# A decoder block on one core: the three joints of the feed-forward part reworked, and one difference moved to GpSimd

## The chip, the core and the metric

The kernel runs on one core of a Trainium2 chip. TensorE multiplies matrices (page name PE, its weight loads PEld), VectorE (DVE), ScalarE (ACT) and GpSimd (POOL) do the elementwise work, SyncE (SP) issues the DMAs. The engines run their own instruction lists and meet only at semaphores. The metric is the device time of one execution in microseconds, lower is better.

## The reference

For x of 16 x 128 x 1024 values in float32, a pre-norm decoder block:

```python
x = x + attn(layernorm(x), Wqkv, q_ln, k_ln, Wout)     # 32 heads, alibi bias, causal, clipped qkv
x = x + xattn(layernorm(x), ctx, Wq, Wk, Wv, Wo, bo, g) # linear attention over channels
W1, W3, W2 = [dequant_q40(w, s) for each]               # two 4-bit values a byte, a scale per group of 64
a = x_n @ W1.T; b = x_n @ W3.T                          # x_n = layernorm(x), 2752 hidden units
x = x + (silu(a) * b) @ W2.T
```

## The kernel before

The program has three phases, each a block of instructions with a barrier behind it: the qkv product, attention (both attentions and Wout, `attention_phase`), and the feed-forward part (`feed_forward_phase`), which the change is about.

Attention goes through the 16 row blocks in turns. Turn b holds the first attention of block b, the second of block b - 1, and the norm, transposes (`post_turn`) and store to `xt` of block b - 2. The last turn, turn 16, has only the second attention of block 15 (`own` is false); the norm and store of block 15 stand behind the turns, and SyncE waits for that store before the block ends.

The feed-forward part splits each float32 operand into a high and a low half and multiplies high by high, high by low and low by high: a product is 12 matmuls of 512 columns. The rows are taken in two halves of 1024. In each half there are 21 whole tiles of 128 hidden units and one merged tile that holds the last 64 units of w1 and w3 together. For a whole tile the 2 by 2 block product is made with seven products instead of eight (A11, S1, S2, A12, S3, S4, A22, in this order): the left operands are blocks and sums of blocks of the weights (GpSimd forms the sums in `left_sums`, ScalarE copies them as high halves into a ring of ten places, DVE subtracts for the low halves), and the right operands b11, t1, t2, b21, t3, b22, t4 are blocks and differences of blocks of the rows, formed once a half (`start_half`, `right_sums`) from `raw`, 4 MB of rows loaded from `xt`. `t1` = R12 - R11 is DVE's, the other three differences are GpSimd's. The merged tile has two products of length 24 and 36 matmuls on b11, t1, b21 and b22. Their places, and those of w2 and of the outputs, lie over one another, so a semaphore guards each reuse.

While TensorE works on tile u, DVE unpacks the weights of tile u + 1 (`unpack13`: two shifts and two scalings), makes its low halves, adds the partial sums of tile u in four `combine`s, and gates. TensorE's second product of tile u + 1 waits for the third `combine` of tile u. After the merged tile of the second half, w2 is loaded and unpacked (`load2`, `unpack2`), split (`w2_high`, `w2_low`), the hidden rows come back from `hid` (`load_hidden`, `hidden_high`, `hidden_low`), `acc` is loaded with the residual rows, and 24 groups of eight output products follow; sum n into `acc` is added by DVE in `add`, and the bank of product n is used again by product n + 8.

Three joints are thus: attention to the first half, first half to second half (in `start_half(1)`), second half to the outputs. The order on each engine is written out by hand.

## Time and profile before

| | |
|---|---|
| median of 3 runs | 3293.26 us (3288.9 to 3293.31) |
| the profiled execution | 3291.72 us, its span 3289.7 us |
| mean granted TensorE clock | 0.968 of full speed |
| busy: PE, DVE, ACT, POOL | 3027.4, 1808.2, 1178.8, 940.9 us |
| first feed-forward load issued | at 1859.12 us |

Busy shares are means over stages with different limits. The stages to look at are the stretches in which TensorE does nothing between two trains of products. A timeline row gives start, duration, engine, line, operation and tiles (output first), the number of instructions merged, and in brackets the idle time before it and what ended it.

### The profile page before, as it was taken

The numbers are of one execution on the slowest core, as the hardware profiler recorded it, in microseconds if no ns is written. First come the engines' busy times: TensorE is split into PE (matmuls) and PEld (weight loads), VectorE is DVE, ScalarE is ACT, GpSimd is POOL, SyncE is SP. The second block draws the span as 40 slices with busy tenths as digits, with TensorE's granted clock in tenths as the row PEclk, the third lists the DMA queues.
The fourth block names the chain that finished last, engine by engine and source line by source line (L and its number), as shares of the span: only waits on it lengthen the run. The fifth ranks groups of instructions, "written<-read, shape, count | busy, mean of one in ns | idle before, by whom it ended". The sixth has DMA issues, their size and how long they took to land. (4 is left out here: it accounts for less than half of the span.)

```text
span 3289.7 us, 40227 instructions
## 1 busy us (share of the span) xinstructions
PE 3027.4 (92%) x14656; PEld 2308.0 (70%) x14656; DVE 1808.2 (55%) x2933; ACT 1178.8 (36%) x2618; POOL 940.9 (29%) x781
## 2 busy tenths in 40 slices
PE   7999998799999999999998389999699996999999
PEld 6888886566666666666655178888588885788887
DVE  5311112466666666666665476665766664455543
ACT  2100000566666665566564233333333332111110
POOL 2100000233333333333343433332533331212221
PEclk9999999899999999999999689999899998999999
DMA  4222222111111111111110222222323224633323
GB/s 144 93 71 74 70 77 101 57 36 48 45 51 46 56 45 54 48 45 45 45 54 30 93 77 84 95 93 77 113 84 103 85 84 116 212 103 94 99 60 119
DMA packets 103341, 256.88 MB, mean 78 GB/s; under 512 B 12352, under 2 KB 18496, under 8 KB 101184
## 3 DMA queue, kind: packets, MB, share of 16 engines
q1 hardware_dynamic: 103232, 255.39, 23.8%
q8 instruction: 72, 1.18, 0.1%
q14 instruction: 37, 0.30, 0.0%
HBM read 181.95 MB, written 73.40 MB: 78 GB/s over the span
## 5 line engine op out<-in xcount | busy, mean ns | idle before, releaser
L1536 PE MATMUL ff_room<-xy,ring_hi 128*128 128x512 f32 x1424 | 358.8, 395 | 40.4 <-DVE xy L1406 25.0
L1536 PEld LDWEIGHTS ff_room<-xy,ring_hi 128*128 128x128 f32 x1424 | 271.3, 191 | 99.1 <-issue 32.9
L284 DVE TENSOR_SCALAR qkv_out<-qkv_acc 128x512 f32<-128x512 f32 x96 | 66.4, 692 | 395.2 <-PE qkv_acc L314 395.2
L1536 PE MATMUL ff_room<-xz,ring_hi 128*128 128x512 f32 x1008 | 252.5, 393 | 29.4 <-DVE xz L1406 29.4
L1445 DVE TENSOR_TENSOR acc<-ff_room,acc 128x512 f32<-128x512 f32 x192 | 130.6, 691 | 227.6 <-PE ff_room L314 220.2
L711 ACT ACTIVATE scores<-scores,neg_max 128x128 f32<-128x128 f32 x512 | 199.2, 390 | 134.0 <-DVE neg_max L496 134.0
L1536 PEld LDWEIGHTS ff_room<-xz,ring_hi 128*128 128x128 f32 x1008 | 191.2, 190 | 70.1 <-issue 30.3
L1410 DVE TENSOR_TENSOR ends<-ends,ff_room 128x512 f32<-128x512 f32 x168 | 115.5, 687 | 212.3 <-ACT ends L1261 198.4
L314 PE MATMUL ff_room<-w_hi,h_hi 128*128 128x512 f32 x704 | 193.4, 393 | 35.2 <-DVE w_lo L1437 28.7
L1226 POOL TENSOR_TENSOR h_lo<-hraw,h_hi 128x2048 fp32r<-128x2048 f32 (+1 forms) x24 | 101.6, 4232 | 413.9 <-ACT h_hi L1322 413.9
L1261 ACT ACTIVATE ends<-ff_room 128x512 f32<-128x512 f32 x126 | 75.3, 598 | 388.4 <-PE ff_room L1536 388.4
L754 POOL TENSOR_TENSOR scores<-scores,row_rec 128x512 f32<-128x512 f32 x128 | 133.3, 1041 | 268.2 <-DVE row_rec L824 268.2
L314 PE MATMUL qkv_acc<-w_hi,xT_hi 128*128 128x512 f32 x768 | 193.0, 394 | 8.9 <-DVE w_lo L257 8.9
L233 ACT ACTIVATE w_hi<-w_stage 128x512 fp32r<-128x512 f32 x56 | 35.4, 632 | 452.9 <-DMA w_stage<-in_w_attn 452.9
L314 PE MATMUL ff_room<-w_lo,h_hi 128*128 128x512 f32 x704 | 192.5, 392 | 0.0
L314 PE MATMUL ff_room<-w_hi,h_lo 128*128 128x512 f32 x704 | 192.5, 392 | 0.0
L1536 PE MATMUL ff_room<-xy,ring_lo 128*128 128x512 f32 x712 | 192.1, 392 | 0.0
L314 PE MATMUL qkv_acc<-w_lo,xT_hi 128*128 128x512 f32 x768 | 190.0, 389 | 0.0
L314 PE MATMUL qkv_acc<-w_hi,xT_lo 128*128 128x512 f32 x768 | 189.8, 389 | 0.0
L314 PEld LDWEIGHTS ff_room<-w_hi,h_hi 128*128 128x128 f32 x704 | 133.9, 191 | 63.8 <-issue 29.0
L1367 DVE TENSOR_SCALAR words<-words,shift 128x1024 int32<-128x1024 int32 (+1 forms) x130 | 143.0, 1113 | 58.5 <-DMA sc<-in_s 43.3
L765 POOL TENSOR_TENSOR qr<-qr,q_rec 128x512 f32<-128x512 f32 x128 | 133.7, 1044 | 139.7 <-DVE q_rec L802 139.7
(179 smaller groups left out, 6260.3 us busy)
## 6 DMA issues: line engine op xcount, KB each, us to landing
words<-in_w SPq DMA_DIRECT2D x86, 512.0 KB, 4.8
qkv<-qkv_out SPq DMA_DIRECT2D x96, 256.0 KB, 2.0
hid<-ends SPq DMA_DIRECT2D x88, 256.0 KB, 3.3
hraw<-hid SPq DMA_DIRECT2D x20, 1024.0 KB, 5.1
qk_in<-qkv SPq DMA_DIRECT2D x16, 1024.0 KB, 4.9
w_stage<-in_w_attn SPq DMA_DIRECT2D x56, 256.0 KB, 3.0
words<-in_w SPq DMA_DIRECT2D x88, 128.0 KB, 3.5
sc<-in_s SPq DMA_DIRECT2D x44, 256.0 KB, 4.0
```

What stands on the lines that cost most here:

```text
L233: nc.scalar.activation(dst[:, r, :], stage[:, r % 2, :], ACT.Copy).then_inc(w_hi_done, 1)
L284: nc.vector.tensor_scalar(res[:, :], acc[:, t % BANKS, :], CLIP, -CLIP, ALU.min, ALU.max).then_inc(clipped, 1)
L314: last = nc.tensor.matmul(out, left, right, start=n == 0, stop=n == len(pairs) - 1)
L711: last = nc.scalar.activation(sc[:, t % SR, j, :], sc[:, t % SR, j, :], ACT.Exp, bias=neg_max[:, t, j:j + 1], accum_out=row_sum[:, t, j:j ...
L754: nc.gpsimd.tensor_tensor(sc[:, n % SR, :, :], sc[:, n % SR, :, :], row_rec[:, n, :].unsqueeze(2).to_broadcast([P, HG, P]), ALU.mult).then ...
L765: nc.gpsimd.tensor_tensor(q, q, q_rec[:, n, :].unsqueeze(2).to_broadcast([P, 8, XD]), ALU.mult).then_inc(s["q_normed"], 1)
L1226: nc.gpsimd.tensor_tensor(flat(h_lo[m % 2][:, 0:n, :]), flat(hraw[m % 2][:, 0:n, :]), flat(h_hi[m % 2][:, 0:n, :]).bitcast(F32), ALU.subtr ...
L1261: nc.scalar.activation(ends[u % 2][:, n, :], chain[u % 2], ACT.Copy).then_inc(s["snapped"], 1)
L1367: last = nc.vector.tensor_scalar(w[:, at], w[:, at], shift[:, 2 * kind:2 * kind + 1], shift[:, 2 * kind + 1:2 * kind + 2], ALU.logical_shi ...
L1410: nc.vector.tensor_tensor(e, e, other, ALU.add).then_inc(s["combined"], 1)
L1445: nc.vector.tensor_tensor(columns(t, n % 2), bank(o), columns(t, n % 2), ALU.add).then_inc(s["added"], 1)
L1536: last = nc.tensor.matmul(out.rearrange("p (a b) -> p a b", a=SETS), l, r, start=not onto and n == 0, stop=n == len(pairs) - 1, skip_group ...
```

## The change

The feed-forward part's helper functions move out of its block. Its first operands are loaded, unpacked and formed in attention's last turn, by `enter_sync`, `enter_gpsimd`, `enter_scalar` and `enter_vector`, which `turn_*` call where `own` is false; attention's tiles are placed anew so that the two do not overlap. The norm, transposes and store of row block 15 move behind that: into the first tiles of the first half (`finish_*`). b11 of the second half has places of its own (`spare`); the merged tile's two products change places; the weights of the second half's first tile are prepared during the tile before the merged one. In the first half all four differences are DVE's; in the second half `t3` is GpSimd's (`difference3_gpsimd`) and the other three DVE's. Of w2's blocks four have a buffer each, and they, the first hidden rows and six `acc` tiles are loaded before the merged tile. High and low left operands share one tile, `ring`. `unpack13`, `left_sums`, `left_high` and `left_low` stay as they were apart from their place in the program. The core of the diff (changes of indentation are left out):

```diff
+        if not own:
+            sp.wait_ge(s["x_done"], 2 * NB)
+            sp.wait_ge(s["xt_stored"], HALF * 16)
+            enter_sync(sp)
...
+            enter_scalar(act, 0)
...
+            enter_gpsimd(pool)
...
-            post_store(sp, NB + 1)
-            sp.wait_ge(s["stored"], (NB + 1) * 16)
-            sp.wait_ge(s["xt_stored"], NB * 16)
...
+    spare = [place(f"xs{i}", [P, SETS, HK, P], F32R, (190 + 8 * i) * KB) for i in range(2)]
...
-    b11, b21, b22, t1 = [(plain[2 * i], plain[2 * i + 1]) for i in range(4)]
-    t2, t3, t4 = (zone[0], zone[1]), (zone[3], zone[5]), (zone[2], zone[4])
-    right = [b11, t1, t2, b21, t3, b22, t4]
+    b11 = [(plain[0], plain[1]), (spare[0], spare[1])]
+    b21, b22, t1 = [(plain[2 * i], plain[2 * i + 1]) for i in range(1, 4)]
+    t2, t3, t4 = (zone[0], zone[1]), (zone[2], zone[5]), (zone[3], zone[4])
...
+    def difference1(dve, hf):
+        for at in (R11, R12):
+            dve.wait_ge(r_in[at - R21], (hf + 1) * 64)
+        nc.vector.tensor_tensor(raw[:, 0, :], raw[:, R12, :], raw[:, R11, :], ALU.subtract).then_inc(s["x_t1"], 1)
+
+    def difference2(dve, hf):
+        dve.wait_ge(s["x_t1"], hf + 1)
+        dve.wait_ge(r_in[R22 - R21], (hf + 1) * 64)
+        nc.vector.tensor_tensor(raw[:, 1, :], raw[:, R22, :], raw[:, 0, :], ALU.subtract).then_inc(s["x_t"], 1)
+
+    def difference4(dve, hf):
+        dve.wait_ge(s["x_t"], 2 * hf + 1)
+        dve.wait_ge(r_in[0], (hf + 1) * 64)
+        nc.vector.tensor_tensor(raw[:, R11, :], raw[:, R21, :], raw[:, 1, :], ALU.subtract).then_inc(s["x_t"], 1)
+
+    def difference3(dve, hf):
+        nc.vector.tensor_tensor(raw[:, R12, :], raw[:, R22, :], raw[:, R12, :], ALU.subtract).then_inc(s["x_t3"], 1)
+
+    def difference3_gpsimd(pool, hf):
+        pool.wait_ge(s["x_t1"], hf + 1)
+        pool.wait_ge(r_in[R22 - R21], (hf + 1) * 64)
+        nc.gpsimd.tensor_tensor(raw[:, R12, :], raw[:, R22, :], raw[:, R12, :], ALU.subtract).then_inc(s["x_t3"], 1)
...
+        op, at = [(b11[hf], R11), (t1, 0), (t2, 1), (b21, R21), (b22, R22), (t3, R12), (t4, R11)][n]
+        if n == 0:
+            act.wait_ge(r_in[R11 - R21], (hf + 1) * 64)
+        elif n == 1:
+            act.wait_ge(s["x_t1"], hf + 1)
+            if hf:
+                act.wait_ge(s["freed"], hf)
+        elif n == 2:
+            act.wait_ge(s["x_t"], 2 * hf + 1)
+            act.wait_ge(s["x_lo"], OPS * hf + 2)
+        elif n == 3:
+            act.wait_ge(r_in[0], (hf + 1) * 64)
+            if hf:
+                act.wait_ge(s["ab_done"], base(hf * NT))
+        elif n == 4:
+            act.wait_ge(r_in[R22 - R21], (hf + 1) * 64)
+            if hf:
+                act.wait_ge(s["ab_done"], base(hf * NT) - 1)
+        elif n == 5:
+            act.wait_ge(s["x_t3"], hf + 1)
+            act.wait_ge(s["x_lo"], OPS * hf + 4)
...
+    def enter_sync(sp):
+        sp.dma_start(shift[:, :], shifts).then_inc(s["shifts"], 16)
+        load13(sp, 0)
+        for at in (R11, R12, R22, R21):
+            load_right(sp, 0, at)
+        load13(sp, 1)
+
+    def enter_gpsimd(pool):
+        left_sums(pool, 0)
+
+    def enter_scalar(act, part):
+        if part == 0:
+            right_high(act, 0, 0)
+            left_high(act, 0, A11)
+            right_high(act, 0, 1)
+        else:
+            right_high(act, 0, 2)
+            left_high(act, 0, S1)
+            right_high(act, 0, 3)
+            right_high(act, 0, 4)
+
+    def enter_vector(dve, part):
+        if part == 0:
+            dve.wait_ge(s["shifts"], 16)
+            unpack13(dve, 0)
+            difference1(dve, 0)
+            left_low(dve, 0, A11)
+            right_low(dve, 0, 0)
+            right_low(dve, 0, 1)
+            difference2(dve, 0)
+        elif part == 1:
+            difference4(dve, 0)
+            right_low(dve, 0, 2)
+        else:
+            left_low(dve, 0, S1)
+            difference3(dve, 0)
...
-                if w >= 2:
-                    sp.wait_ge(s["w2_done"], w - 1)
+                    i = buffer2(w)
+                    if w >= 4:
+                        sp.wait_ge(s["w2_done"], w - 3 if w < 6 else w - 1)
+                    elif w >= 2:
+                        sp.wait_ge(s["w_lo"], base(TILES - 1))
+                    else:
+                        sp.wait_ge(s["ab_done"], base(NT))
...
+                for u in range(1, TILES):
                     if u + 1 < TILES:
-                    load13(u + 1)
-                if u:
+                        load13(sp, u + 1)
+                    if u == 3:
+                        finish_sync(sp)
+                    if u == WHOLE:
+                        finished(sp)
+                        sp.wait_ge(s["ab_done"], base(WHOLE))
+                        load_right(sp, 1, R11)
+                        load_right(sp, 1, R12)
                     store(u - 1)
-                if u == NT - 1:
-                    load_right(1)
-            sp.wait_ge(s["ab_done"], base(TILES - 1))
+                    if u == WHOLE:
+                        load_right(sp, 1, R22)
+                        load_right(sp, 1, R21)
+                    if u == NT + 2:
                         load2(0)
                         load2(1)
-            load_hidden(0)
+                    if u == TILES - 2:
                         load2(2)
                         load2(3)
+                        load_hidden(0)
+                        sp.wait_ge(s["ab_done"], base(TILES - 1))
+                        for t in range(6):
+                            load_acc(t)
                 store(TILES - 1)
-            load_hidden(1)
                 sp.wait_ge(s["ab_done"], base(TILES))
-            for t in range(NB):
-                sp.dma_start(acc[:, t, :], x2[t, :, :]).then_inc(acc_in[t // SETS], 16)
+                for t in range(6, 10):
+                    load_acc(t)
...
+                load_hidden(1)
+                for parity in range(2):
+                    sp.wait_ge(h_stored[parity], stored_before(TILES, parity))
+                for t in range(10, NB):
+                    load_acc(t)
                 for m in range(CHUNKS2 * SETS):
...
-            for hf in range(2):
-                left_sums(hf * NT)
-                right_sums(hf)
-                for u in range(hf * NT, hf * NT + WHOLE):
+                for u in range(TILES):
+                    if merged(u):
+                        continue
                     if not merged(u + 1):
-                        left_sums(u + 1)
+                        left_sums(pool, u + 1)
+                    elif u + 2 < TILES:
+                        left_sums(pool, u + 2)
                     gate(u)
+                    if u == WHOLE - 1:
+                        difference3_gpsimd(pool, 1)
+                    if u == 0:
+                        finish_gpsimd(pool)
...
+                    if u == 0:
+                        for j in (S2, A12, S3):
+                            left_high(act, 0, j)
+                        snap(0, 0)
+                        right_high(act, 0, 5)
+                        left_high(act, 0, S4)
+                        left_high(act, 0, A22)
+                        snap(0, 1)
+                        right_high(act, 0, 6)
+                        left_high(act, 1, A11)
+                    elif u == NT:
+                        right_high(act, 1, 0)
+                        silu_merged(WHOLE, 0)
+                        right_high(act, 1, 1)
+                        silu_merged(WHOLE, 1)
                         snap(u, 0)
-                    if merged(v):
-                        left_high(v, 0)
-                        left_high(v, 1)
+                        right_high(act, 1, 2)
+                        right_high(act, 1, 3)
+                        right_high(act, 1, 4)
+                        snap(u, 1)
+                        right_high(act, 1, 5)
+                        right_high(act, 1, 6)
+                        left_high(act, v, A11)
...
+                    if u == 0:
+                        left_low(dve, 0, S2)
+                        right_low(dve, 0, 3)
+                        left_low(dve, 0, A12)
+                        right_low(dve, 0, 4)
+                        left_low(dve, 0, S3)
+                        right_low(dve, 0, 5)
+                        left_low(dve, 0, S4)
+                        left_low(dve, 0, A22)
+                        right_low(dve, 0, 6)
+                        finish_vector(dve)
+                    elif u == NT:
+                        difference1(dve, 1)
+                        right_low(dve, 1, 0)
+                        gate_merged(WHOLE, 0)
+                        right_low(dve, 1, 1)
+                        difference2(dve, 1)
+                        gate_merged(WHOLE, 1)
+                        difference4(dve, 1)
+                        right_low(dve, 1, 2)
+                        right_low(dve, 1, 3)
+                        right_low(dve, 1, 4)
+                        right_low(dve, 1, 5)
+                        right_low(dve, 1, 6)
...
+                    elif v + 1 < TILES:
+                        unpack13(dve, v + 1)
+                        for j in (A11, S1, S2):
+                            left_low(dve, v + 1, j)
...
+                    else:
+                        unpack2(2)
                     gate(u)
-                if hf == 0:
-                    unpack13(NT)
-                    gate_merged(WHOLE, 0)
-                    gate_merged(WHOLE, 1)
-                    start_half(1)
+                    if merged(v) and v + 1 < TILES:
+                        left_low(dve, v + 1, A22)
+                    if u == TILES - 4:
                         unpack2(0)
+                    if u == TILES - 3:
                         unpack2(1)
-            gate_merged(TILES - 1, 0)
+                unpack2(3)
                 w2_low(0)
                 w2_low(1)
-            unpack2(2)
-            gate_merged(TILES - 1, 1)
-            unpack2(3)
                 w2_low(2)
+                gate_merged(TILES - 1, 0)
                 w2_low(3)
+                gate_merged(TILES - 1, 1)
...
                 def merged_tile(u):
+                    hf = u // NT
                     pe.wait_ge(s["w_lo"], base(u) + 2)
-                pe.wait_ge(s["h0_done"], u - 1)
-                multiply(chain[u % 2], terms(u, 0, b11) + terms(u, 1, b21))
                     pe.wait_ge(s["combined"], 4 * whole_before(u) - 2)
-                multiply(bank_b, terms(u, 0, t1) + terms(u, 0, b11) + terms(u, 1, b22))
+                    multiply(bank_b, terms(u, 0, t1) + terms(u, 0, b11[hf]) + terms(u, 1, b22), used=3 * HK)
+                    pe.wait_ge(s["h0_done"], u - 1)
+                    multiply(chain[u % 2], terms(u, 0, b11[hf]) + terms(u, 1, b21))
...
+                    if u == 1:
+                        finish_tensor(pe, rows_bank)
```

DVE's list from its last two steps of attention on, before: `n_sq` and `xn` belong to the second attention's norm, `v_in` is its scaling, `x_st` the statistics of row block 15.

```order
L864 TENSOR_SCALAR n_sq<-pair_k 128x8
L866 TENSOR_TENSOR xn<-ident,n_sq 128x1024
L882 TENSOR_TENSOR v_in<-v_in,bank_q 128x512
L882 TENSOR_TENSOR v_in<-v_in,bank_d 128x512
L503 BN_STATS x_st<-res 128x6
```

The same place of the change, from the first difference of `raw` on, which follows the unpacking of the weights' `words`:

```order
L1225 TENSOR_TENSOR raw<-raw 128x2048
L1216 TENSOR_TENSOR ring<-words,ring 128x512
L1277 TENSOR_TENSOR xy<-raw,xy 128x2048 x2
L1230 TENSOR_TENSOR raw<-raw 128x2048
L888 TENSOR_SCALAR n_sq<-pair_k 128x8
L890 TENSOR_TENSOR xn<-ident,n_sq 128x1024
L1235 TENSOR_TENSOR raw<-raw 128x2048
L1277 TENSOR_TENSOR xz<-raw,xz 128x2048
L908 TENSOR_TENSOR v_in<-v_in,bank_q 128x512
L908 TENSOR_TENSOR v_in<-v_in,bank_d 128x512
```

Two differences and three low halves (`xy`, `ring`) now stand ahead of `n_sq`, a difference and a low half (`xz`) between it and the scaling.

DVE's list where the first half ends, before: `ends` are the gates of the merged tile, `raw` the first difference of the second half, `xy` and `xz` low halves of right operands.

```order
L1423 MEMSET ends 64x512
L1424 TENSOR_TENSOR ends<-ends,ff_room 64x512
L1423 MEMSET ends 64x512
L1424 TENSOR_TENSOR ends<-ends,ff_room 64x512
L1400 TENSOR_TENSOR raw<-raw 128x2048
L1394 TENSOR_TENSOR ring_lo<-words,ring_hi 128x512
L1406 TENSOR_TENSOR xy<-raw,xy 128x2048 x2
L1394 TENSOR_TENSOR ring_lo<-sums,ring_hi 128x512 x2
L1406 TENSOR_TENSOR xz<-raw,xz 128x2048
```

And now, with `xs` the spare place:

```order
L1225 TENSOR_TENSOR raw<-raw 128x2048
L1277 TENSOR_TENSOR xs<-raw,xs 128x2048
L1563 MEMSET ends 64x512
L1564 TENSOR_TENSOR ends<-ends,ff_room 64x512
L1277 TENSOR_TENSOR xy<-raw,xy 128x2048
L1230 TENSOR_TENSOR raw<-raw 128x2048
L1563 MEMSET ends 64x512
L1564 TENSOR_TENSOR ends<-ends,ff_room 64x512
L1235 TENSOR_TENSOR raw<-raw 128x2048
L1277 TENSOR_TENSOR xz<-raw,xz 128x2048
L1277 TENSOR_TENSOR xy<-raw,xy 128x2048 x2
L1277 TENSOR_TENSOR xz<-raw,xz 128x2048 x2
```

A difference and a low half come ahead of both gates, and two more differences stand between the low halves.

SyncE's list before the outputs, before: `hid` are the merged tile's stores, `hraw` the hidden rows, `x` the residual rows, `words_0` and `sc_0` w2's fifth block; w2's first four blocks (24 issues) stand ahead of these rows.

```order
L1120 DMA hid<-ends 128x512
L1125 DMA hid<-ends 128x512
L1148 DMA hraw<-hid 128x4x512
L1172 DMA acc<-x 128x1024 x16
L1132 DMA words_0<-in_w 64x512
L1133 DMA words_0<-in_w 64x512
```

And now, from the first hidden rows on, with w2's first four blocks again ahead of them, but in the tiles before:

```order
L1360 DMA hraw<-hid 128x4x512
L1365 DMA acc<-x 128x1024 x6
L1326 DMA hid<-ends 128x512
L1331 DMA hid<-ends 128x512
L1326 DMA hid<-ends 128x512
L1331 DMA hid<-ends 128x512
L1365 DMA acc<-x 128x1024 x4
L1360 DMA hraw<-hid 128x4x512
L1365 DMA acc<-x 128x1024 x6
L1344 DMA words_0<-in_w 64x512
```

Six tiles of `acc` are loaded before the merged tile's stores, and the second hidden rows come behind four more.

## Rows read from the trace of the kernel before

**Rows 1.** The chain of waits, feed-forward phase: start us, us, what.
```profile
1907.57 410.84 PE ff_room L1536 x1800
...
2355.28 396.96 PE ff_room L1536 x1740
...
2807.29 18.31 DMA sc<-in_s
...
2828.55 457.36 PE ff_room L314 x2004
```

**Rows 2.** Who waited for whom, TensorE, 1790 to 2870: us in total, times, longest.
```profile
PE ff_room L1536 <- DVE xz L1406: 29.4, 2, 18.1
PE ff_room L314 <- DVE w_lo L1437: 28.7, 1, 28.7
PE ff_room L1536 <- DVE xy L1406: 25.0, 1, 25.0
...
PE ff_room L1536 <- DVE ring_lo L1394: 8.2, 2, 5.9
...
PE ff_room L314 <- DVE acc L1445: 6.5, 1, 6.5
```

**Rows 3.** Timeline of TensorE, first tile: start, us, engine, line, op.
```profile
1915.67 1.98 PE L1536 MATMUL ff_room<-xz,ring_hi 128*128 128x512 f32 x8
...
1918.39 1.98 PE L1536 MATMUL ff_room<-xy,ring_hi 128*128 128x512 f32 x8
```

**Rows 4.** Timeline of DVE, attention's last turn.
```profile
1821.96 0.20 DVE L802 RECIPROCAL q_rec<-q_sum 128x8 f32<-128x8 f32 x1
1837.70 0.17 DVE L864 TENSOR_SCALAR n_sq<-pair_k 128x8 f32<-128x8 f32 x1 [15.53 <-PE pair_k L679]
...
1845.41 0.68 DVE L882 TENSOR_TENSOR v_in<-v_in,bank_d 128x512 f32<-128x512 f32 x1
```

**Rows 5.** Windows: stretch, busy PE, PEld, DVE, ACT, POOL; granted clock, DMA share, GB/s.
```profile
1907.00:1912.00 5.00, 4.43 (x11) 3.53 (x12) 4.97 (x5) 0.74 (x2) 0.00 (x0) 0.50 0.51 175
...
2804.00:2826.00 22.00, 18.05 (x80) 14.62 (x78) 0.37 (x1) 0.00 (x0) 0.00 (x0) 0.96 1.04 325
```

**Rows 6.** Timeline of SyncE's DMA issues, attention's end and the next block.
```profile
1796.44 0.34 SPq L555 DMA_DIRECT2D x<-res  x1
...
1855.70 0.33 SPq L533 DMA_DIRECT2D xt<-x2t  x1
1859.12 0.35 SPq L1102 DMA_DIRECT2D words<-in_w  x1
```

**Rows 7.** Timeline of SyncE's DMA issues, start of the outputs.
```profile
2790.68 12.55 SPq L1172 DMA_DIRECT2D acc<-x  x16
```

**Rows 8.** Instructions of the tiles `xy`: ns min/median/max, first and last start.
```profile
L1254 ACT ACTIVATE xy<-raw x8: 1893/1897/1911, 1868.8 to 2335.6; 128x2048 fp32r<-128x2048 f32 x8
L1406 DVE TENSOR_TENSOR xy<-raw,xy x8: 2274/2280/6629, 1876.1 to 2342.5; 128x2048 fp32r<-128x2048 f32 x8
```

**Rows 9.** Timeline of DVE, start of the second half.
```profile
2327.51 10.03 DVE L1394 TENSOR_TENSOR ring_lo<-sums,ring_hi 128x512 fp32r<-128x512 f32 x2
...
2357.29 0.81 DVE L1367 TENSOR_SCALAR words<-words,shift 128x1024 int32<-128x1024 int32 x1
...
2361.26 0.68 DVE L1394 TENSOR_TENSOR ring_lo<-words,ring_hi 128x512 fp32r<-128x512 f32 x1
...
2368.35 0.68 DVE L1410 TENSOR_TENSOR ends<-ends,ff_room 128x512 f32<-128x512 f32 x1
```

**Rows 10.** Timeline of GpSimd, attention's last turn and the block after.
```profile
1846.23 2.34 POOL L785 TENSOR_TENSOR res<-v_in,res 128x1024 f32<-128x1024 f32 x1 [6.63 <-DVE v_in L882]
...
1869.76 1.26 POOL L1195 TENSOR_TENSOR sums<-words 128x512 f32<-128x512 f32 x1 [17.23 <-DVE words L1389]
```

**Rows 11.** Timeline of GpSimd, start of the second half.
```profile
2332.07 4.92 POOL L1212 TENSOR_TENSOR raw<-raw 128x2048 f32<-128x2048 f32 x1
```

**Rows 12.** Timeline of DVE, w2's low halves.
```profile
2791.90 2.43 DVE L1437 TENSOR_TENSOR w_lo<-words,w_hi 128x1024 fp32r<-128x1024 f32 x2
```

943 lines of the change are left out of this document (459 added, 484 removed).

## Prediction

> **What bounds the kernel now.** Read the chain of waits first. From the start of the feed-forward phase on, it is TensorE with holes: three trains of products, 410.84, 396.96 and 457.36 us long, and between them stretches with other names on the chain [rows 1]. The waits of TensorE name the same holes: 29.4 us for low halves of operands (`xz`), 28.7 for w2's low halves, 25.0 for `xy`, 8.2 for `ring_lo`, 6.5 for a sum into `acc` [rows 2]. Inside a train nothing waits: a product of 12 matmuls follows the next every 2.72 us (1915.67 to 1918.39) [rows 3]. So the phase is bound by TensorE inside the trains and by the joints between them, and I cost only the joints.
>
> One unit helps: a half has 21 tiles of 7 products and a merged tile worth 5, 152 products or 413.4 us; the outputs are 176 products (2112 matmuls), 478.7 us. From these and [rows 1], what each joint loses against full speed:
> - joint 1 (attention to first half): the first train ends at 1907.57 + 410.84 = 2318.41. DVE's last work of attention's inner loop ends at 1822.16 [rows 4], a point that the change does not move. 2318.41 - 1822.16 - 413.4 = 82.8 us lost.
> - joint 2: the second train ends at 2752.24, plus 13.6 for the merged tile is 2765.84. 2765.84 - 2318.41 - 413.4 = 34.0 us lost.
> - joint 3: outputs end at 2828.55 + 457.36 = 3285.91. 3285.91 - 2765.84 - 478.7 = 41.4 us lost.
> A start after a wait has a price of its own: the first two products from 1907.57 take 8.10 us to 1915.67 instead of 5.44, 2.66 us more, while the granted clock is 0.50, the lower level of 1.2 GHz [rows 1, 3, 5].
>
> **Joint 1 after the change.** What is removed: the barrier no longer waits for the last row block's statistics, transposes and store, and none of the loads and splits stand behind it (the first load is issued at 1859.12 now) [rows 6]. What is added to the last turn:
> - SyncE: 23 loads right after the store at 1796.44. At 0.35 us (the issue at 1859.12) to 0.78 an issue (12.55 for 16) [rows 6, 7] they are out by 1805 to 1815, before DVE wants them at 1822. The store of the row block before goes behind them and nobody waits for it. I cost the loads at nothing; DVE's and ScalarE's idle time in this turn is the cover.
> - DVE, part 0 (from 1822.16): unpack 3.97 (2357.29 to 2361.26), two differences and two low halves at 2.28 each, one small low half 0.68 [rows 8, 9]: 13.8 us, to 1835.9. GpSimd's four sums, 1.26 each [rows 10], want the same stretch.
> - Do they lie beside each other? The trace says no. A GpSimd op of 4.92 us ran at 2332.07, and two small DVE ops that cost 0.68 apiece took 10.03 from 2327.51 [rows 9, 11]: one engine stands while the other reads two SBUF tiles. The Trainium skill (SBUF — State Buffer, section "SBUF: two separate sides") states this as an exclusive lock on a port pair that the two share; the trace agrees, 10.03 against 1.3; by it the 5.0 below counts in full, without it the first product would come 3.2 earlier.
>  So I add the 5.0 us of sums in full: `n_sq`, now at 1837.70 [rows 4], comes at 1840.9, 3.2 late (bounds 0 and 5).
> - DVE, part 1: 4.6 us of work in a wait of 3.9 (the scaling's first half is at about 1844.8, a 0.68 op ahead of 1845.41) [rows 4, 8]: 0.6 late. `v_in` ends at 1846.1 + 3.8 = 1849.9. Then GpSimd's 2.34 [rows 10] and DVE's 0.68 + 2.28 take turns, to 1855.2. A new block costs under 3.4 us (1855.70 to 1859.12, a store's landing included) [rows 6]; I take 0.7. First product at 1855.9 (bounds 1851 and 1860).
> After that, the first tile still forms operands. DVE has four low halves and five small ones; the last one's ScalarE half sits behind a copy that waits for the third product, 2.66 + 8.16 = 10.8 after the start; with the copy (0.6, an estimate from a third of 1.90), the 1.90 conversion and 2.28 it is done at 15.6, and the moved statistics (about 1.9, three small ops) end at 17.5. From the next unpack to its third sum 11.74 us pass (2357.29 to 2369.03) [rows 8, 9], so 29.2. TensorE wants that sum at 24.7 (7 products, 2.66, 0.25 wait for the first operand, one product): 4.6 us stall; perhaps a slow start again, half of 2.66. The moved transposes cost 1.0 on TensorE (eight, each at most a 0.227 us matmul: bound 1.8). First half ends at 1855.9 + 413.4 + 2.7 + 4.6 + 1.3 + 1.0 = 2278.9. **Gain 39.5** (bounds 30 and 49).
>
> **Joint 2.** Removed: two of three GpSimd differences of 2048 columns, and the wait of the first operand's place for the merged tile (the spare place). The second half's first seven left operands are made during the tile before; that is 15.5 us for DVE (one and a half unpacks of 3.97, fourteen ops of 0.68) and 5.0 of GpSimd's sums, in a tile of 19.04 and the first 9 of the merged one, where DVE has nothing else; I cost it at nothing, and without this cover it would be the 11.74 of a tile's preparation. From the merged tile's start (0; its end is 13.6): eight load issues and a landing put the first difference's end at about 9 (bounds 8 and 11). Low half 11.3, gate 12.4. Here GpSimd's difference, 4.92, gets the port; the next low half ends at 18.2, and the second product, wanted at 16.3, waits 1.9. Then a difference, a gate, a difference and a low half, 8.0 us, end at 26.2 against 20.9: 5.3. The sixth low half waits for a copy behind the third product: 33.7 against 31.6: 2.1. Its last unit ends at 36.0, plus 11.74 is 47.7, against 44.6: 3.1. With one slow start 2.7: 15.1 us lost instead of 34.0. **Gain 18.9** (bounds 8 and 27).
>
> **Joint 3.** With w2's first four blocks and the hidden rows loaded before, what is left from the merged tile's start is five ScalarE conversions of at most 1.90, four low halves of 1.2 (2.43 for two) and one GpSimd op of 4.92 [rows 8, 11, 12]; the last low half stands behind the gate of the first merged product (8.16 + 1.2) and ends near 11.5, before 13.6. The 28.7 us wait [rows 2] goes. What is late next: the tenth output product, 24.5 after, needs a sum that stands on DVE behind the fifth block's unpack, and that block's loads stand behind `acc` tiles. Now the last of them takes 18.31 us to land at 2825.60, 34.9 after the first `acc` issue [rows 1, 7], with the DMA engines full at 325 GB/s [rows 5]. Ten `acc` tiles instead of 16 save 3.1 MB, 9.7 us; from 2.5 that lands at 27.7, less if the hidden rows come later; with unpack and sum 2.9: up to 6 us stall. I take 5.0 and a slow start, 7.7 lost instead of 41.4. **Gain 33.7** (bounds 27 and 41).
>
> **Sum.** 39.5 + 18.9 + 33.7 = 92.1. The profiled execution took 3291.72 (span 3289.7), so 3199.6, say 3200; the median of the runs, 3293.26, lies 1.5 above it, within their own spread, and I add nothing.
>
> **Rivals.**
> - The shared port eats joint 2. For it: 10.03 for two small ops [rows 9]. If the difference on GpSimd holds DVE twice, or waits out DVE's train and is itself late for its conversion, joint 2 loses about 12 more: 3212. Chance 0.12. The Trainium skill (Perfetto Trace Analysis, section "Optimizing Scalar/DVE Operations") says that moving work between these two engines might not help because of this port; the rows bear it out for the three differences, and by it the GpSimd difference brings nothing over DVE's 2.28 us.
> - The last turn grows. For it: DVE's 13.8 and GpSimd's 5.0 stand ahead of `n_sq`; if ScalarE's halves come late too, the first product moves by 12, to 1868: 3212. Against: DVE is idle there for 15 us (1822.16 to 1837.70) [rows 4]. Chance 0.10.
> - The change does not do what it says in joint 1: the 23 loads land only around 1845, and unpacking waits. Joint 1 gains 15: 3224. Against: 325 GB/s moves their 6 MB in 19 us [rows 5]. Chance 0.06.
> - Better: the stalls of joints 2 and 3 fall into covered time, 25 us: 3175. Chance 0.14.
> - Slower: high and low left operands now interleave in one tile. If the weight load from it took so long that a product needed more than 2.72 us, 480 products decide: from 0.19 us each (2.91) the whole gain is gone; at 0.25 the time is 3320. Against: nothing in the trace shows such a dependence. Chance 0.03.
>
> **How the numbers follow.** My forecast, 3190 to 3212 by its own bounds, has 0.55. The range 3176 to 3224 takes in the rivals of 3212, most of the 3224 and the 3175 ones, and leaves out the last; about 0.85. A time within 0.2% (6.6 us) of now cannot be told from no change; only a mixture of the last rival with the forecast falls there: 0.01. Faster 0.96, slower 0.03.
>
> **What would show it.** Right: the first `ff_room` product at 1851 to 1860; the TensorE wait of 28.7 us for `w_lo` gone, with matmuls from the merged tile straight into the outputs; one GpSimd op on `raw` of 5 us or more at the second half's start, with a stretched DVE op beside it; a hole of 0 to 7 us about 24 us into the outputs; products still every 2.72 us. Wrong: `n_sq` more than 5 us late; a wait for `raw` loads in the last turn; a hole of more than 8 us in joint 2.

## The result and the profile after

The changed kernel takes 3210.22 us (median of 4 runs, 3209.94 to 3210.66) against 3292.95 us of the kernel before (4 runs, 3288.9 to 3293.31): a ratio of 0.9752, 95% interval 0.9735 to 0.9769, 82.7 us less. 3200 was forecast, with a range of 3176 to 3224; the forecast's own range was 3190 to 3212. The profiled execution took 3210.66 with a span of 3208.9, 80.8 less than the span before.

The joints are measured as in the prediction: from the end of DVE's work in attention's inner loop (now 1817.86 + 0.20 = 1818.06), less the products at 2.72 us each.

| loss at (us) | before | forecast | after | gain forecast | gain measured |
|---|---|---|---|---|---|
| ahead of joint 1 | | | | 0 | 4.1 |
| joint 1 | 82.8 | 43.3 | 46.8 | 39.5 | 36.0 |
| joint 2 | 34.0 | 15.1 | 24.6 | 18.9 | 9.4 |
| joint 3 | 41.4 | 7.7 | 10.2 | 33.7 | 31.2 |
| sum | | | | 92.1 | 80.7 |

The chain of waits of the changed kernel, rows that answer to [rows 1] (start us, us, what). The trains of products are longer, the holes between them shorter:

```profile
1851.19 9.95 PE ff_room L1691 x36
...
1878.38 23.60 PE ff_room L1691 x96
...
1902.86 375.39 PE ff_room L1691 x1656
...
2316.00 383.91 PE ff_room L1691 x1680
...
2729.64 16.60 DMA sc<-in_s
...
2749.19 455.93 PE ff_room L324 x2004
```

What TensorE waited for between 1790 and 2870 us, answering to [rows 2]: the 28.7 us for w2's low halves are 0.8, the 29.4 and 25.0 for right operands are gone under these names. New are waits for ScalarE's copies (`ends`), and what the view calls issue, which in the second half's start is the wait for right operands (below):

```profile
PE ff_room L1691 <- ACT ends L1448: 13.4, 2, 9.1
PE ff_room L1691 <- issue: 9.9, 4, 3.4
...
PE ff_room L324 <- DVE acc L1587: 7.4, 1, 7.4
...
PE ff_room L324 <- DVE w_lo L1578: 0.8, 1, 0.8
```

The first tile on TensorE, a timeline as in [rows 3]. The sixth product starts at 1866.41 and would end at 1869.13; the seventh starts 9.1 us later. Between waits a product still takes 2.72 us (1888.21 to 1890.93), so high and low halves interleaved in one tile cost nothing:

```profile
1866.41 2.88 PE L1691 MATMUL ff_room<-xy,ring 128*128 128x512 f32 x12
1878.38 4.54 PE L1691 MATMUL ff_room<-xz,ring 128*128 128x512 f32 x12 [9.09 <-ACT ends L1448]
...
1888.21 2.88 PE L1691 MATMUL ff_room<-xz,ring 128*128 128x512 f32 x12
1890.93 2.88 PE L1691 MATMUL ff_room<-xy,ring 128*128 128x512 f32 x12
```

ScalarE at that place, a timeline. The last row is the copy that the seventh product waits for. Ahead of it stand high halves for the second tile (`ring`), which wait for its unpacked weights (DVE) and sums (POOL), and a silu with its table load:

```profile
1861.17 0.60 ACT L1448 ACTIVATE ends<-ff_room 128x512 f32<-128x512 f32 x1 [2.01 <-PE ff_room L1691]
...
1869.60 0.63 ACT L1211 ACTIVATE ring<-words 128x512 fp32r<-128x512 f32 x1 [6.03 <-DVE words L1185]
1873.31 0.63 ACT L1211 ACTIVATE ring<-sums 128x512 fp32r<-128x512 f32 x1 [3.08 <-POOL sums L1195]
1874.66 0.63 ACT L1211 ACTIVATE ring<-sums 128x512 fp32r<-128x512 f32 x1 [0.72 <-POOL sums L1197]
...
1875.83 1.28 ACT L1453 ACT_TABLE_LOAD   x1
1877.12 0.63 ACT L1453 ACTIVATE ends<-ends 128x512 f32<-128x512 f32 x1
1877.66 0.58 ACT L1448 ACTIVATE ends<-ff_room 128x512 f32<-128x512 f32 x1
```

DVE and GpSimd in attention's last turn (timelines of each), answering to [rows 4, 10]. Two low halves take 6.62 instead of 4.6 us (twice 2.28), GpSimd's sums 3.3 instead of 1.26, while they run beside each other. `n_sq` comes 1837.01 - 1818.06 = 19.0 us after the inner loop, 3.4 later than the 15.5 before:

```profile
1817.86 0.20 DVE L824 RECIPROCAL q_rec<-q_sum 128x8 f32<-128x8 f32 x1
...
1826.55 6.62 DVE L1277 TENSOR_TENSOR xy<-raw,xy 128x2048 fp32r<-128x2048 f32 x2
...
1837.01 0.17 DVE L888 TENSOR_SCALAR n_sq<-pair_k 128x8 f32<-128x8 f32 x1 [0.56 <-PE pair_k L695]
...
1845.09 0.68 DVE L908 TENSOR_TENSOR v_in<-v_in,bank_d 128x512 f32<-128x512 f32 x1
```

```profile
1822.89 3.19 POOL L1195 TENSOR_TENSOR sums<-words 128x512 f32<-128x512 f32 x1 [3.21 <-DVE words L1185]
...
1830.99 3.31 POOL L1200 TENSOR_TENSOR sums<-words,sums 128x512 f32<-128x512 f32 x1
```

The start of the second half on TensorE, DVE and GpSimd (timelines), answering to [rows 9, 11]. The first half ends at 2278.25, its merged tile begins 13.6 us earlier, at 2264.65. DVE's first difference waits 3.92 us for its rows to be loaded. Five of the first seven products wait, and each of the five then takes 4.4 to 5.5 us instead of 2.9. The second, at 2287.19, starts 0.11 us after the end of DVE's low half in the rows under it (2281.79 + 5.29):

```profile
2280.62 4.58 PE L1691 MATMUL ff_room<-xs,ring 128*128 128x512 f32 x12 [2.37 <-issue]
2287.19 4.58 PE L1691 MATMUL ff_room<-xy,ring 128*128 128x512 f32 x12 [1.98 <-issue]
2295.15 4.39 PE L1691 MATMUL ff_room<-xz,ring 128*128 128x512 f32 x12 [3.37 <-issue]
...
2304.40 4.59 PE L1691 MATMUL ff_room<-xz,ring 128*128 128x512 f32 x12 [2.13 <-issue]
...
2316.00 5.46 PE L1691 MATMUL ff_room<-xz,ring 128*128 128x512 f32 x12 [4.29 <-ACT ends L1448]
```

```profile
2276.03 2.29 DVE L1225 TENSOR_TENSOR raw<-raw 128x2048 f32<-128x2048 f32 x1 [3.92 <-DMA raw<-xt]
...
2281.79 5.29 DVE L1277 TENSOR_TENSOR xy<-raw,xy 128x2048 fp32r<-128x2048 f32 x1
```

```profile
2279.40 5.53 POOL L1243 TENSOR_TENSOR raw<-raw 128x2048 f32<-128x2048 f32 x1 [7.84 <-DMA raw<-xt]
```

### The profile page after: what moved, and what is told of

Read it like the earlier page. It is cut to its first block and busy times, and to the rows that moved or that the text cites. A ratio compares the mean times of both kernels' runs of the same rounds, so it can differ in the third digit from the quotient of the medians.

```text
span 3208.9 us, 40226 instructions
## 1 busy us (share of the span) xinstructions
PE 3019.4 (94%) x14656; PEld 2305.2 (72%) x14656; DVE 1810.1 (56%) x2938; ACT 1178.8 (37%) x2618; POOL 908.0 (28%) x776
## 5 line engine op out<-in xcount | busy, mean ns | idle before, releaser
L1691 PE MATMUL ff_room<-xy,ring 128*128 128x512 f32 x1860 | 446.2, 391 | 9.2 <-PEq L924 7.2
L1691 PEld LDWEIGHTS ff_room<-xy,ring 128*128 128x128 f32 x1860 | 351.1, 189 | 84.4 <-issue 11.1
L1691 PE MATMUL ff_room<-xz,ring 128*128 128x512 f32 x1512 | 370.6, 395 | 18.9 <-ACT ends L1448 13.4
L1691 PEld LDWEIGHTS ff_room<-xz,ring 128*128 128x128 f32 x1512 | 288.5, 191 | 80.9 <-issue 15.8
L324 PEld LDWEIGHTS qkv_acc<-w_hi,xT_hi 128*128 128x128 f32 x768 | 144.1, 189 | 38.7 <-DVE w_lo L267 9.4
L324 PEld LDWEIGHTS qkv_acc<-w_lo,xT_hi 128*128 128x128 f32 x768 | 144.6, 188 | 30.3
L324 PEld LDWEIGHTS qkv_acc<-w_hi,xT_lo 128*128 128x128 f32 x768 | 144.1, 188 | 29.9
```

The lines of the kernel that those rows point to most:

```text
L324: last = nc.tensor.matmul(out, left, right, start=n == 0, stop=n == len(pairs) - 1)
L1691: last = nc.tensor.matmul(out.rearrange("p (a b) -> p a b", a=SETS), l, r, start=not onto and n == 0, stop=n == len(pairs) - 1, skip_group ...
```

## Experiments

Each ratio is to the kernel before, timed beside the run. The median of the kernel before moved by up to 1.9 us between these timings (3291.01 to 3292.95), so as a time a difference of 3 us from the changed kernel (ratio 0.9752) is weak. Where the difference is small, the joint's loss in the profiled execution is given, worked out as in the table above.

**The third copy first.** In the first tile of each half, ScalarE copies the chain bank (in which a tile's first, third, fifth and seventh products add up) for the third time before it turns to the next tile's high halves.

```diff
                         right_high(act, 0, 6)
+                        snap(0, 2)
                         left_high(act, 1, A11)
...
                         right_high(act, 1, 6)
+                        snap(u, 2)
                         left_high(act, v, A11)
...
                     silu(u, 0)
-                    snap(u, 2)
+                    if u % NT:
+                        snap(u, 2)
```

> ScalarE's third copy of the chain bank stands ahead of the next tile's high halves in the first tile of each half; nothing else moves. Theory A (the seventh product waits only because this copy is queued behind high halves that wait for sums of the next tile): the stalls of 9.1 us (first half) and 4.3 us (second half) before the seventh product go; what is late next is DVE's third sum, which holds the next tile's second product by about 4.6 us in the first half and 1 us in the second. Some 8 to 11 us less with the clock's share: 3199 to 3203. Rival (DVE's train of unpacking and low halves sets the pace, the copy is only the last in it): the same stall stands before the next product instead, 3208 to 3212.

Measured: 3202.73 us, ratio 0.9730 (0.9714 to 0.9746). TensorE's timeline of this run: the seventh product now starts behind the sixth, and the second product of the next tile waits for DVE's third sum.

```profile
1870.01 2.88 PE L1694 MATMUL ff_room<-xz,ring 128*128 128x512 f32 x12
...
1880.20 5.46 PE L1694 MATMUL ff_room<-xy,ring 128*128 128x512 f32 x12 [4.10 <-DVE ends L1554]
```

The 4.10 us are the stall that the prediction had put there (4.6); joint 1 loses 43.5 instead of 46.8. Theory A: the copy's place in ScalarE's order was a stall of its own, ahead of the one forecast. In the second half the wait for the third sum was 2.7, not 1. Joint 2 loses 19.0 instead of 24.6, but that is not the copy's alone: the rows of the second half also landed some 2 us sooner in this execution, as they did in the third experiment, which leaves the copy where it was and loses 22.7.

**The second half's difference on DVE.** This is `t3`, the difference that the title speaks of. It was GpSimd's in the kernel before as well, with two others; the change took those two to DVE and left this one where it was, so nothing was moved to GpSimd. Here it goes to DVE too.

```diff
-                    if u == WHOLE - 1:
-                        difference3_gpsimd(pool, 1)
...
                         right_low(dve, 1, 2)
+                        difference3(dve, 1)
                         right_low(dve, 1, 3)
```

> The second half's third difference goes from GpSimd back to DVE, behind the low half of the third operand. Theory A (GpSimd's 5.53 us op stretches one DVE low half from 2.28 to 5.29 us and that delay reaches the third product): the low half is back at 2.3 us, the third product's wait of 3.4 us falls to about 0.5, 2 to 5 us less: 3205 to 3208. Rival of the prediction (the shared port eats joint 2): 12 us less, 3198. Rival C (the first difference waits for its load, so the rest is hidden by that, and DVE pays its own 2.3 us): no change, 3209 to 3212.

Measured: 3207.21 us, ratio 0.9744 (0.9728 to 0.9760). DVE's low half beside which GpSimd worked is back from 5.29 to 2.28 us, and no difference is stretched in its place. But the third product still waits 4.95 us, not the 0.5 of theory A (timelines of DVE and TensorE):

```profile
2273.83 2.29 DVE L1225 TENSOR_TENSOR raw<-raw 128x2048 f32<-128x2048 f32 x1 [2.07 <-DMA raw<-xt]
...
2279.60 2.28 DVE L1277 TENSOR_TENSOR xy<-raw,xy 128x2048 fp32r<-128x2048 f32 x1
...
2285.35 2.28 DVE L1235 TENSOR_TENSOR raw<-raw 128x2048 f32<-128x2048 f32 x1
```

```profile
2289.93 5.07 PE L1690 MATMUL ff_room<-xz,ring 128*128 128x512 f32 x12 [4.95 <-issue]
```

The waits move with the time at which the rows land, which differs by some 2 us between executions. What does not move with it is the stretch from DVE's first difference to the third product: 19.1 us in the changed kernel (2295.15 - 2276.03), 16.1 here (2289.93 - 2273.83). In the run of the third experiment, which leaves this place as it is and in which the rows came as soon as here, it is 19.1 again (from 2275.44), although another DVE operation was the stretched one (the third difference, 5.28 us from 2286.97; TensorE's timeline of that run):

```profile
2294.55 5.46 PE L1693 MATMUL ff_room<-xz,ring 128*128 128x512 f32 x12 [7.96 <-issue]
```

So GpSimd's difference delays the third product by 3.0 us. Joint 2 loses 19.2 us, against 22.7 in that run and 22.6 in the run with joint 1's forming undone (below): the difference on GpSimd costs about 3.5 us and gains nothing. (The changed kernel loses 24.6, but there the rows came 2 us later.) By the size this is theory A, though its wait of 0.5 was missed; the rival of the prediction, 12 us, is not seen. The Trainium skill (Perfetto Trace Analysis, section "Optimizing Scalar/DVE Operations") says that work moved between these two engines might not help, because they share a read port; the trace agrees, 5.53 us on GpSimd and 3.0 us more on DVE for an op that takes DVE 2.28.

**w2's fifth block before `acc`.**

```diff
                 load_hidden(1)
+                load2(4)
+                load_hidden(2)
...
                 for t in range(10, NB):
                     load_acc(t)
```

> The loads of w2's fifth block and of the third hidden rows are issued before the last six tiles of acc instead of behind them. Theory A (the hole of 7.4 us in the outputs is the fifth block's scales landing 16.6 us after their issue because 3 MB of acc are ahead of them): the hole goes, with about 2 us of slow clock: 3200 to 3203. Rival (the DMA engines are full, so the hole only moves to the next thing loaded, the sixth block or acc's third group): 3206 to 3211 with a hole of 4 to 7 us later in the outputs.

Measured: 3200.23 us, ratio 0.9723 (0.9707 to 0.9739). TensorE waits for nothing in the outputs but the first 0.8 us; joint 3 loses 1.1 instead of 10.2. Theory A.

**One part of the rows earlier.**

```diff
-                        sp.wait_ge(s["ab_done"], base(WHOLE))
-                        load_right(sp, 1, R11)
-                        load_right(sp, 1, R12)
+                        sp.wait_ge(s["ab_done"], base(WHOLE) - 2)
+                        load_right(sp, 1, R12)
+                        sp.wait_ge(s["ab_done"], base(WHOLE))
+                        load_right(sp, 1, R11)
```

> One of the four parts of the rows for the second half is loaded when its place comes free, two products earlier (5.4 us); the other three as before. Theory A (joint 2 begins 3.9 us late because its first difference waits for this part's load): the first difference starts at about 2272.5 instead of 2276.0, the first product's wait of 2.4 us goes with its slow clock of 1.9: 3204 to 3207. Rival (what follows, the GpSimd difference and the low halves, is set by other loads and the port): the first wait goes but the next ones grow by as much, 3209 to 3211.

Measured: 3206.75 us, ratio 0.9744 (0.9728 to 0.9760). Both were half right. The first difference no longer waits (it starts at 2270.16), and the first two products follow without a gap. But the third waits 7.48 instead of 3.37 us: it starts 19.1 us after the first difference, as in the changed kernel, with GpSimd's difference and one of DVE's side by side in that stretch (timelines of TensorE, GpSimd and DVE):

```profile
2276.20 2.88 PE L1692 MATMUL ff_room<-xs,ring 128*128 128x512 f32 x12
2278.92 2.88 PE L1692 MATMUL ff_room<-xy,ring 128*128 128x512 f32 x12
2289.28 4.88 PE L1692 MATMUL ff_room<-xz,ring 128*128 128x512 f32 x12 [7.48 <-issue]
```

```profile
2276.85 7.97 POOL L1243 TENSOR_TENSOR raw<-raw 128x2048 f32<-128x2048 f32 x1 [7.16 <-DMA raw<-xt]
```

```profile
2281.67 5.30 DVE L1235 TENSOR_TENSOR raw<-raw 128x2048 f32<-128x2048 f32 x1
```

The waits of joint 2 add up to 13.8 us, against 14.1; its loss falls from 24.6 to 19.7. What is saved against the changed kernel is the slow products behind the two waits that went. Not all of it is the edit's: in the run of the third experiment the rows came sooner without it, those two products were not slow either, and joint 2 lost 22.7. Against that run the edit saves 3.0 us.

**The places of attention's tiles alone.** The kernel before, with the tiles of attention declared in the order of the changed kernel:

```diff
     bias = sb("alibi", [P, HEADS, P], F32, ph)
-    rel = sb("rel", [P, P], F32, ph)
-    ones = sb("ones", [P, P], F32, ph)
...
+    kD = sb("kD", [P, G, HG, P], F32, ph)
+    kT = sb("kT", [P, KT, XO], F32, ph)
...
```

> The kernel before, with attention's tiles in the order of the changed kernel and nothing else. The changed kernel reached the end of attention's inner loop 4.1 us sooner, 0.24 us of it in each of 14 turns (75.48 instead of 75.72 us from store to store). Theory A (the places of attention's tiles shorten the turn): 75.5 us a turn here too, 3287 to 3290. Rival (it is the spread between executions): 75.7 us a turn, the time of the kernel before, 3289 to 3293.

Measured: 3286.97 us, ratio 0.9986 (0.9977 to 0.9995). SyncE's stores of the first and the last of these turns (timeline of the issues) are 14 turns apart, (1792.51 - 735.73) / 14 = 75.48 us:

```profile
735.73 0.43 SPq L555 DMA_DIRECT2D x<-res  x1
```

```profile
1792.51 0.34 SPq L555 DMA_DIRECT2D x<-res  x1
```

The inner loop ends at 1818.91 in this run, 3.3 us sooner than before. In the profiles of the changed kernel and of all runs made from it, it ends between 1815.57 and 1819.06. So theory A: most of the 4.1 us ahead of joint 1 come from the places, and the rest lies within that spread. Which tile does it was not tried.

**Joint 1's forming undone.** The operands are loaded and formed at the start of the feed-forward block; the last row block stays behind them.

```diff
         if not own:
-            sp.wait_ge(s["x_done"], 2 * NB)
-            sp.wait_ge(s["xt_stored"], HALF * 16)
-            enter_sync(sp)
...
             @block.sync
             def _(sp):
+                enter_sync(sp)
...
+                for part in range(3):
+                    enter_vector(dve, part)
```

> The changed kernel with the first operands loaded and formed at the start of the feed-forward block instead of in attention's last turn; the last row block's norm and store stay behind that. Theory A (forming the operands in the last turn is most of joint 1's gain): the first load is issued at about 1851, the first product follows some 48 us later as it did before, near 1899; the stall before the seventh product stays; 3250 to 3262. Rival (most of the gain is that the barrier no longer waits for the last row block): the first product near 1865, 3220 to 3228.

Measured: 3233.9 us (one run). The first product starts at 1866.19, 20.4 us after the first load at 1845.84, not 48. The 48 was a misreading: in the kernel before, the first product was at 1879.61, 20.5 after the first load; 1907.57, where the prediction let its train begin, is the third product. Joint 1 loses 70.4 us here. So of the 36.0 us gained, 12.4 come without the last turn (the barrier that no longer waits for the last row block, and the new order of the operands), and 23.6 with it. Neither theory's time was met; by these shares, which rest on one profile, theory A's statement holds. The run also shows what the forming costs in the last turn: `n_sq` comes 1833.89 - 1818.28 = 15.6 us after the inner loop when no operand is formed beside it, 19.0 when they are.

**All mended.** The edits of the first four experiments together; beside them the last row block's statistics behind the first tile on DVE, in each first tile the third sum ahead of two low halves and one right high half ahead of ScalarE's second copy, and the second merged gate behind the third operand's low half. The core:

```diff
                         right_low(dve, 0, 6)
-                        finish_vector(dve)
...
+                    if u % NT == 0:
+                        dve.wait_ge(s["snapped"], k + 3)
+                        combine(u, 2, 2, bank_c)
                     if not merged(v):
                         left_low(dve, v, S2)
...
                     gate(u)
+                    if u == 0:
+                        finish_vector(dve)
...
                         left_high(act, 0, A22)
+                        right_high(act, 0, 6)
                         snap(0, 1)
-                        right_high(act, 0, 6)
+                        snap(0, 2)
                         left_high(act, 1, A11)
```

> The changed kernel with the four edits together (third copy early, second half's difference on DVE, w2's fifth block before acc, one part of the rows loaded early), and the last row block's statistics behind the first tile on DVE, the third sum ahead of two low halves in each first tile, the last high half ahead of a copy, the second merged gate behind the third operand's low half. Theory A (the stalls are independent queues' orders): seventh-product stalls and the hole gone, third product's wait about 3 us, fifth's about 3; joint losses about 36, 10 and 1 us: 3172 to 3182. Rival (one DVE and one load queue carry them all, so mending one lengthens another): the gains of 7.5, 3, 10 and 3.5 do not add up, 3188 to 3195.

Measured: 3179.08 us (5 runs, 3178.64 to 3180.74), ratio 0.9659 (0.9645 to 0.9672): 31 us faster than the changed kernel. The joints lose 38.0, 11.0 and 1.1 us, close to the 36, 10 and 1 of theory A, and the rival is out: the gains add up. The four edits alone had given 7.5, 3.0, 10.0 and 3.5 us, 24 together; the other 7 come with the further edits, which were not tried one by one. The chain's last two rows are one train to the end of the second half and one through the outputs:

```profile
2304.48 372.92 PE ff_room L1701 x1644
...
2694.51 479.01 PE ff_room L324 x2112
```

**Fillers in the waits.** Matmuls into an unused bank before the waited-for products.

```diff
                     for j in range(OPS):
+                        for _ in range({(0, A22): 28, (NT, A11): 7, (NT, S1): 5, (NT, S2): 10, (NT, S3): 6,
+                                        (NT, A22): 14}.get((u, j), 0)):
+                            nc.tensor.matmul(room[:, 7, :].rearrange("p (a b) -> p a b", a=SETS), b11[0][0][:, 0, 0, :],
+                                             b11[0][0][:, :, 0, :], start=True, stop=True)
                         pe.wait_ge(s["w_lo"], base(u) + j + 1)
```

> The changed kernel with matmuls into an unused bank put where TensorE waits (28 before the first half's seventh product; 7, 5, 10, 6 and 14 before five products of the second half's first tile); their results are not used. Theory A (after each wait the next product runs at the lower clock, about 2 us each, because TensorE stood idle): the granted clock stays at 1.00 in these products, they take 2.72 us again; 3199 to 3204. Rival (the clock falls for another reason, or the fillers hold up the products they stand ahead of): 3208 to 3214.

Measured: 3208.17 us, ratio 0.9747 (0.9732 to 0.9762); as a time, inconclusive. The rows show why: 2.80 us of the 9.1 were left unfilled, and the product behind them was slow all the same. Yet the second half's second product, behind 2.40 us left unfilled, was not slow (2.97 us). The fillers were made longer:

> As the filler run before, with the fillers made longer where a wait of more than 2 us was left behind them (38, 12, 20, 8 and 24 instead of 28, 5, 10, 6 and 14; the first stays 7). Theory A (the lower clock follows TensorE's idle time, so a wait that is filled up to under 1 us costs no slow product): both seventh products and the third one take 2.7 to 2.9 us instead of 4.3 to 4.4; some 5 us less than the changed kernel, 3203 to 3206. Rival (the fillers only push the products they stand ahead of): 3208 to 3212.

Measured: 3204.04 us, ratio 0.9735 (0.9720 to 0.9750), theory A. TensorE's timelines of the two runs, the fillers and the seventh product behind them:

```profile
1867.99 6.51 PE L1709 MATMUL ff_room<-xy 128*128 128x512 f32 x28
1877.30 4.50 PE L1691 MATMUL ff_room<-xz,ring 128*128 128x512 f32 x12 [2.80 <-ACT ends L1448]
```

```profile
1868.65 8.77 PE L1708 MATMUL ff_room<-xy 128*128 128x512 f32 x38
1877.96 2.98 PE L1691 MATMUL ff_room<-xz,ring 128*128 128x512 f32 x12 [0.54 <-ACT ends L1448]
```

The wait is as long (the product starts 9.3 us after the sixth ends in both), but behind 0.54 us of idle time it takes 2.8 us, behind 2.80 it takes 4.3. Joint 2 loses 18.9, against 22.5 with the short fillers and 24.6 in the changed kernel.

Fillers in the two long waits of the mended version, 12 and 11 matmuls before the second half's third and fifth products, by the same edit:

> The version with all mended edits (3179.1) and fillers of 12 and 11 matmuls in its two waits of 3.2 and 3.1 us, ahead of the second half's third and fifth products; their results are not used. Theory A (the lower clock follows the idle time): both products take 2.8 us instead of 4.2, some 3 us less: 3175 to 3177. Rival: no change, 3178 to 3181.

Measured: 3182.80 us (5 runs, 3181.53 to 3186.85), ratio 0.9670 (0.9657 to 0.9683), not faster than without; both expectations missed. The two products do take 2.8 us, but the fifth starts 19.2 us after the half's start instead of 19.0: DVE's operands set that time. The seventh product's wait for ScalarE's copy grew from 1.09 to 2.25 us and it ran slow, so joint 2 loses 12.9 instead of 11.0. In this profile, which is of the slowest of the five executions, joint 3 also lost 4.7 us more, 2.7 of it a wait for the second hidden rows, which the mended version leaves 0.4 us of room. Whether fillers cause either was not tried.

## Why the prediction was right, and where its terms were off

- **What bounds the kernel.** Right: apart from attention's turns (below) only the joints moved, and the trains run at 2.72 us a product as before. The rival of slower weight loads is out.
- **Joint 1 up to the first product.** Right, to 0.6 us: 33.1 us after the inner loop (1851.19 - 1818.06), where 33.7 was forecast (1855.9 - 1822.16). The loads were free, DVE's unpacking followed the inner loop at once, and with DVE's operands and GpSimd's sums in one stretch, each stretching the other, `n_sq` came 3.4 late where 3.2 was forecast.
- **Joint 1, the stall.** The term "4.6 us stall" was mis-sized: 9.1 and a slow product of 1.7. I took DVE's third sum as the first thing late and did not follow ScalarE's own order, in which the copy that the seventh product needs stands behind high halves of the next tile. In a running half these halves rarely wait (15 of all 298 high halves of left operands waited for weights or sums); in a first tile they do. The third sum is the next limit, at 4.1 us, as the first experiment shows.
- **Joint 2.** This step failed by half: a loss of 24.6 instead of 15.1. Two terms were mis-sized. The first is the load: the first difference was to end about 9 us after the merged tile's start (bounds 8 and 11), and it ended 13.7 after it (2278.32 - 2264.65), 11.6 in the run with the third copy first. From there DVE's train kept to the forecast: the third product, forecast at 26.2, started at 30.5. The second is "one slow start 2.7": five products were slow, 10.5 us in all. The long fillers show that idle time ahead of them is the cause, and give 3.6 to 5.7 us back (22.5 with short fillers, or 24.6 without, to 18.9). That the waits were near in sum, 14.1 instead of 12.4 us, is luck in part. One by one they were 2.4, 2.0, 3.4, 2.1 and 4.3, where the forecast had 0, 1.9, 5.3, 2.1 and 3.1, and the last pair is not the same wait: the 3.1 was for DVE's third sum, ahead of the next tile's second product, and the 4.3 is the seventh product's for ScalarE's copy, overlooked here as in joint 1. With the copy first, the third sum cost 2.7.
- **The shared port.** Right in kind: one DVE operation took 5.29 us instead of 2.28 beside GpSimd's difference. The row of 10.03 was read too simply: its two small operations stood beside two GpSimd operations, the one of 4.92 and one of 9.33 that began at 2322.66.
- **Joint 3.** Right in mechanism: a hole of 7.4 us (5.0 forecast) at the tenth output product, behind w2's fifth block behind `acc`, removed by the third experiment together with its slow clock.
- **The inner loop's end** as "a point that the change does not move" was wrong by 4.1 us, mostly because the new places of attention's tiles shorten its turns.
- **The sum.** Joint 2 fell short by 9.5, joint 1 by 3.5 and joint 3 by 2.5, and 4.1 came in unforeseen: 80.7 instead of 92.1. Those 4.1 are luck: without them the time would be about 3214, outside the forecast's own 3190 to 3212. The range of 3176 to 3224 was said to take in the rival of 3175, which lies 1 us below it. The time lies near the 3212 of two rivals, but neither happened: the difference on GpSimd cost about 3.5 us, not 12, and the last turn grew by 4.0 us to its store (30.5 us after the inner loop, 26.5 in the run with the forming undone), not 12.

## What to carry to other kernels

Where work is moved ahead so that a pipeline starts sooner, walk through the order of every engine for the first round: a copy or a sum that stands behind the next round's work is free in the steady state and a stall in the first one. Allow for a slow product behind each wait, not for one at each joint: five short waits close together cost here three quarters as much again as they lasted (10.5 beside 14.1), though not every short wait was followed by one. And a wait that an earlier load removes may only move on, when the next operand is made by the same two engines.

## What the runs showed of the hardware

- Idle time costs TensorE twice, but not by its length alone: behind a wait of 2.13 us a product took 4.43 us from start to start in the changed kernel, granted clock 0.63 there, and 2.82 in the run with the third copy first, behind a wait of the same 2.13. Why stays open. The two windows and that product (window: us, busy PE, PEld, DVE, ACT, POOL, granted clock, DMA share, GB/s):

```profile
2304.40:2309.00 4.60, 4.60 (x13) 3.65 (x14) 4.57 (x4) 0.48 (x1) 0.00 (x0) 0.63 0.02 4
```

```profile
2300.70:2304.00 3.30, 3.23 (x14) 2.73 (x15) 3.27 (x3) 0.21 (x1) 0.00 (x0) 1.00 0.00 0
```

```profile
2300.77 2.99 PE L1694 MATMUL ff_room<-xz,ring 128*128 128x512 f32 x12 [2.13 <-issue]
```

- The order in which attention's tiles are declared, with every instruction the same, took 0.24 us from each turn of 75.72 (one profile of each; the medians of all runs differ by 4.8 us). Why stays open.
